# Expert stage of a retention and mixture-of-experts kernel: tile pairs outside, Strassen up projection, transposed down projection

## What is computed

```python
x = _layernorm(x + retention_stack(x))            # (8, 512, 256)
logits = xt @ Wr + br                             # xt: (4096, 256)
gates = entmax_bisect(logits)                     # (4096, 8)
gates = where(gates > THRESH, gates, 0)
h = relu(einsum('td,edf->etf', xt, W1) + b1[:, None, :])   # f = 1024
y = einsum('etf,efd->etd', h, W2) + b2[:, None, :]
out = einsum('etd,te->td', y, gates)
x = _layernorm(x + out)
```

## Time and profile before

| | |
|---|---|
| median of 3 runs | 2757.17 us (2754.56 to 2759.98) |
| profiled execution, span | 2757.3 us |
| expert stage, from its first instruction | 1210.8 us to the end |
| TensorE busy, share of the span | 95% |
| VectorE, ScalarE, GpSimd busy | 49%, 49%, 47% |
| matmuls | 14962 |
| mean TensorE clock granted | 0.975 of full |

### The profile page before, as it was taken

The page is one execution under the profiler, slowest core; times in us unless marked ns, Lnnn a source line. Parts: engine busy times, 40 slices in busy tenths (PEclk is TensorE's granted clock), DMA queues, the critical chain, the costliest instruction groups (busy, mean ns, idle before and its releaser), DMA issues.

```text
span 2757.3 us, 42999 instructions
## 1 busy us (share of the span) xinstructions
PE 2625.7 (95%) x14962; PEld 2292.4 (83%) x14962; DVE 1348.6 (49%) x2432; ACT 1361.9 (49%) x2246; POOL 1301.5 (47%) x1142
## 2 busy tenths in 40 slices
PE   7999999999999999949899999999999999999998
PEld 5788778877888788738798998989989989899997
DVE  2677887777777877757812112121121121211233
ACT  3555555566556555525344444444444444444443
POOL 2244554455445544435345445454454454544454
PEclk8999999999999999966999999999999999999999
DMA  4110020002000100042001001000010000000000
GB/s 153 58 31 30 31 69 31 30 31 69 31 30 31 38 31 23 15 133 70 31 0 33 0 0 33 0 29 5 0 34 0 0 33 0 2 0 0 8 23 31
DMA packets 70774, 82.77 MB, mean 30 GB/s; under 512 B 3104, under 2 KB 65696, under 8 KB 70688
## 3 DMA queue, kind: packets, MB, share of 16 engines
q1 hardware_dynamic: 70560, 81.58, 9.0%
q10 hardware_dynamic: 128, 0.03, 0.0%
HBM read 58.27 MB, written 23.33 MB: 30 GB/s over the span
## 4 chain that ended last, share of the span: by engine, by line
issue 24%; POOL 17%; PE 13%; POOLq 1%; DVE 0%; DMA 0%; ACT 0%; ACTq 0%; DVEq 0%; SPq 0%
POOL hid_lo L1257 17%; PE m_ps L1500 4%; PE m_ps L1501 4%; PE m_ps L1502 4%; DMA xh<-h_store 0%; POOLq L1256 0%; PE m_ps L1519 0%; PE m_ps L1526 0%; DVE x L1358 0%; POOLq L1260 0%; ACT x1T_hi L1302 0%; ACT x1Tf L1301 0%; DVE xh L1370 0%; DVE m_stat L1347 0%; POOL rstd L1236 0%
## 5 line engine op out<-in xcount | busy, mean ns | idle before, releaser
L1257 POOL TENSOR_TENSOR hid_lo<-act,hid_hi 128x512 fp32r<-128x512 f32 x512 | 701.5, 1372 | 759.6 <-ACT act L1329 759.5
L1327 ACT ACTIVATE hid_hi<-m_ps,b_e 128x512 fp32r<-128x512 f32 x512 | 353.4, 690 | 811.4 <-PE m_ps L1502 811.2
L1444 DVE TENSOR_TENSOR tile_out<-m_ps,b_bc 128x512 f32<-128x512 f32 x128 | 82.4, 686 | 1015.9 <-PE m_ps L1502 1015.6
L1329 ACT ACTIVATE act<-m_ps,b_e 128x512 f32<-128x512 f32 x512 | 349.7, 683 | 0.0
L1500 PE MATMUL m_ps<-w_even,hid_hi 128*128 128x256 f32 x1024 | 289.6, 283 | 13.5 <-DVE tile_out L1444 13.0
L1502 PE MATMUL m_ps<-w_even,hid_lo 128*128 128x256 f32 x1024 | 290.3, 284 | 0.0
L1501 PE MATMUL m_ps<-w_even,hid_hi 128*128 128x256 f32 x1024 | 290.3, 283 | 0.0
L1500 PE MATMUL m_ps<-w_odd,hid_hi 128*128 128x256 f32 x1024 | 289.1, 282 | 0.8 <-POOL hid_lo L1257 0.6
L1502 PE MATMUL m_ps<-w_odd,hid_lo 128*128 128x256 f32 x1024 | 289.7, 283 | 0.0
L1501 PE MATMUL m_ps<-w_odd,hid_hi 128*128 128x256 f32 x1024 | 289.6, 283 | 0.0
L320 POOL TENSOR_TENSOR pf_lo<-tmp,pf_hi 128x512 fp32r<-128x512 f32 x128 | 161.8, 1298 | 159.4 <-ACT pf_hi L497 159.4
(11 more groups left out here) (176 smaller groups left out, 6305.4 us busy)
## 6 DMA issues: line engine op xcount, KB each, us to landing
h_store<-h_out SPq DMA_DIRECT2D x32, 512.0 KB, 3.2
raw<-in_L_ffn_W SPq DMA_DIRECT2D x16, 1024.0 KB, 6.8
h_in<-h_store SPq DMA_DIRECT2D x24, 512.0 KB, 4.3
h_in<-in_L_attn_x SPq DMA_DIRECT2D x8, 512.0 KB, 5.0
raw<-in_L_attn_Wf SPq DMA_DIRECT2D x8, 512.0 KB, 7.6
acc<-in_L_attn_x SPq DMA_DIRECT2D x8, 512.0 KB, 4.2
xh<-h_store SPq DMA_DIRECT2D x8, 512.0 KB, 5.0
out<-acc SPq DMA_DIRECT2D x8, 512.0 KB, 2.8
```

The lines of the kernel that those rows point to most:

```text
L1257: nc.gpsimd.tensor_tensor(out=hid[1][:, j % RING, :], in0=act32[:, j % FULL, :], in1=f32(hid[0][:, j % RING, :]), op=ALU.subtract).then_in ...
L1327: nc.scalar.activation(hid[0][:, j % RING, :], hid_bank(j), ACT.Relu, bias=bias)
L1329: nc.scalar.activation(act32[:, j % FULL, :], hid_bank(j), ACT.Relu, bias=bias).then_inc(hid_relu, 1)
L1444: nc.vector.tensor_tensor(out=tile_out[:, 2 * half:2 * half + 2, :], in0=out_half(parity_t, half).rearrange("p (k d) -> p k d", d=D), in1= ...
```

## The change

Only the expert stage changes (the semaphores of the weight halves in the retention layers become one count, in the same order of work). Four pairs of tiles run outside and the eight experts inside. A step, a "quad", is one pair of tiles, one expert and two hidden chunks: 128 quads in all, QPP = 32 for a pair, FP = 4 for an expert. The four blocks of a quad (two chunks by two tiles, each a sum over two halves of 128 features) come out of seven products instead of eight, after Strassen in the form of Winograd:

- of the weights VectorE makes four sums S1 to S4 of 128 by 128 (`sum_weights`) in the buffer into which they were loaded, ScalarE rounds 11 blocks (1408 columns) in one copy (`high_weights`), VectorE subtracts (`low_weights`); this is done for every quad, so for every pair of tiles again;
- of the tokens four sums T1 to T4 are made once for a pair (`sum_tokens`), with seven high and seven low halves;
- three banks take the products. ScalarE copies the first product to `first` (`keep_first`), VectorE makes `second` and `third` and three of the four blocks (`second_sum`, `third_sum`, `block_sum`), each from one PSUM bank and one SBUF tile;
- ReLU runs twice per block on ScalarE (`relu`), from PSUM for block C11 and from SBUF for C22, C21 and C12, and GpSimd subtracts (`low_hidden`);
- `down` has the weights stationary and the 512 columns of the hidden block moving: 24 matmuls of 512 columns for a quad, with features on the output's partitions;
- the gate must then be a row over tokens: the gates are transposed, stored to memory and loaded as broadcast rows (`gate_bc`). VectorE adds the bias and multiplies (`gate_out`), GpSimd adds into `acc` (`add_expert`), one of 512 columns for each quad on the mean;
- moments, transposes, scores and the 25 bisection steps of the next pair run inside the windows of the present one; for the first pair, four steps come ahead and three in each of the first seven windows.

Window w issues the products of quad w+1 between the down projections of quad w. The diff, shortened, with all that the prediction speaks of; first two helpers of VectorE:

```diff
-            for j in range(AHEAD):
-                up(w1[0], 0, 0, j)
-            for e in range(2):
-                expert(e, e)
...
+            def sum_weights(q):
...
+                one = chained(nc.vector.tensor_tensor(out=part(8), in0=part(0), in1=part(2), op=ALU.add))
+                nc.vector.tensor_tensor(out=part(10), in0=part(1), in1=part(0), op=ALU.subtract)
+                dve.wait_ge(dve_done, one)
+                landed(nc.vector.tensor_tensor(out=part(9), in0=part(8), in1=part(1), op=ALU.subtract))
+                nc.vector.tensor_tensor(out=part(11), in0=part(3), in1=part(9), op=ALU.subtract).then_inc(w_summed, 1)
...
+            def block_sum(q, k):
+                p, e, fp = quad(q)
+                done, src, other, made = {C22: (4, bank_d, third, 2), C21: (6, bank_b, first, 3), C12: (7, bank_d, second, 4)}[k]
+                dve.wait_ge(up_done, 7 * q + done)
...
+                nc.vector.scalar_tensor_tensor(out=full[:, k, :], in0=src, scalar=b1_col(e, 2 * fp + BLOCK_ROW[k]), in1=other[:, :],
+                                               op0=ALU.add, op1=ALU.add).then_inc(sums, 1)
```

The loop over windows on VectorE:

```diff
+            for w in range(-1, QUADS):
+                p, i = w // QPP, w % QPP
+                if w >= 0 and w % FP == 0 and w:
+                    for j in (2, 3):
+                        gate_out(w // FP - 1, j)
+                if w + 1 < QUADS:
+                    second_sum(w + 1)
+                if w + 3 < QUADS:
+                    low_weights(w + 3)
+                if w < CLOSED:
+                    bisect(EARLY + PER_WINDOW * (w + 1) + 1)
...
+                if w + 1 < QUADS:
+                    third_sum(w + 1)
+                    block_sum(w + 1, C22)
+                if w + 4 < QUADS:
+                    sum_weights(w + 4)
+                if w < CLOSED:
+                    for n in range(2, PER_WINDOW + 1):
+                        bisect(EARLY + PER_WINDOW * (w + 1) + n)
...
+                    if 18 <= i < 31:
+                        bisect(2 * (i - 18) + 1)
...
+                if w >= 0 and w % FP == FP - 1:
+                    for j in (0, 1):
+                        gate_out(w // FP, j)
+                if w + 1 < QUADS:
+                    block_sum(w + 1, C21)
+                    block_sum(w + 1, C12)
```

The same on ScalarE, in the same loop:

```diff
+                if w + 3 < QUADS:
+                    high_weights(w + 3)
+                if w + 1 < QUADS:
+                    keep_first(w + 1)
+                if w >= 0:
+                    relu(w, C12)
...
+                if w + 1 < QUADS:
+                    for k in (C11, C22, C21):
+                        relu(w + 1, k)
```

On GpSimd:

```diff
+                if w >= 0:
+                    low_hidden(w, C12)
...
+                if w >= FP * 2:
+                    add_expert(w // FP - 1, w % FP)
+                if w + 1 < QUADS:
+                    for k in (C11, C22, C21):
+                        low_hidden(w + 1, k)
```

On TensorE, where a product of quad w+1 stands ahead of each down projection of quad w, and then the waits inside `product`:

```diff
+                for n in range(5):
+                    if ups:
+                        product(w + 1, n)
+                    if downs:
+                        down(w, n // 2, n % 2)
...
+                    down(w, C21, 1)
+                if ups:
+                    product(w + 1, 5)
+                if downs:
+                    down(w, C12, 0)
+                if ups:
+                    product(w + 1, 6)
+                if downs:
+                    down(w, C12, 1)
...
+                if n in (1, 2) and q:
+                    pe.wait_ge(sums, 5 * (q - 1) + 3 + n)
+                if n == 3:
+                    pe.wait_ge(sums, 5 * q + 1)
```

More of the change, by code:

```diff
@@ new lines, in expert_mixture @@
+        t_sum = sb("t_sum", [P, 4, S])
+        acc = [sb(f"m_acc{s}", [P, DC, 2 * S]) for s in range(2)]
+        gate_bc = [sb(f"gate_bc{s}", [P, 2 * S]) for s in range(2)]
+        gate_first = sb("gate_first", [P, 2 * S])
+        hid_hi, hid_lo = (sb(f"hid_{n}", [P, 4, S], F32R) for n in ("hi", "lo"))
+        first, second, third = (sb(f"sum{n}", [P, S]) for n in range(3))
+        full = sb("full", [P, 4, S])
+        gated = sb("gated", [P, 4, S])
+        xs, hs = (sb(f"m_{n}s", [P, 2, TB, D]) for n in ("x", "h"))
@@ new lines, in add_expert @@
+            def add_expert(n, j):
+                at = acc[n // E % 2][:, j % 2, (j // 2) * S:(j // 2 + 1) * S]
+                if n == 1:
+                    pool.wait_ge(first_added, j + 1)
+                else:
+                    pool.wait_ge(acc_added, added(n - 1, j))
+                pool.wait_ge(out_gated, 4 * n + j + 1)
+                nc.gpsimd.tensor_tensor(out=at, in0=at, in1=gated[:, j, :], op=ALU.add).then_inc(acc_added, 1)
+            for t in range(2):
+                inverse_root(t)
@@ new lines, in relu @@
+            def relu(q, k):
+                p, e, fp = quad(q)
+                bias = b1_col(e, 2 * fp + BLOCK_ROW[k])
+                if k == C11:
+                    act.wait_ge(up_done, 7 * q + 5)
+                    src = bank_a
+                else:
+                    act.wait_ge(sums, 5 * q + {C22: 3, C21: 4, C12: 5}[k])
+                    src = full[:, k, :]
+                if q:
+                    act.wait_ge(hid_used, 4 * (q - 1) + k + 1)
+                if k == C11:
+                    nc.scalar.activation(hid_hi[:, k, :], src, ACT.Relu, bias=bias)
+                    if q:
+                        act.wait_ge(hid_ready, 4 * (q - 1) + k + 1)
+                    nc.scalar.activation(full[:, k, :], src, ACT.Relu, bias=bias).then_inc(relu_ready, 1)
+                else:
+                    nc.scalar.activation(hid_hi[:, k, :], src, ACT.Relu)
+                    nc.scalar.activation(full[:, k, :], src, ACT.Relu).then_inc(relu_ready, 1)
@@ L1400, in each @@
+            mx, lo, total, step = (tau[:, n, :] for n in range(4))
+            SPAN = 1.0 - float(E) ** -0.5
             def each(v):
                 return v.unsqueeze(2).to_broadcast([P, NB, E])
-            fixed = B * TILE_CHAIN
-            count[0] = 0
-            mx, lo, total, above, sign, step, tot = (ent_s[:, i, :] for i in range(7))
-            scores, work = gates[:, :, :], ent_w
-            SPAN = 1.0 - float(E) ** -0.5
-            def rowsum_of_squares(ahead):
-                landed(nc.vector.scalar_tensor_tensor(out=work, in0=scores, scalar=ahead, in1=each(lo), op0=ALU.subtract, op1=ALU.subtract), fixed)
-                landed(nc.vector.scalar_tensor_tensor(out=work, in0=work, scalar=0.0, in1=work, op0=ALU.max, op1=ALU.mult), fixed)
-                landed(nc.vector.tensor_reduce(out=total, in_=work, op=ALU.add, axis=AX.X), fixed)
@@ new lines, in second_sum, with third_sum @@
+            def second_sum(q):
+                dve.wait_ge(up_done, 7 * q + 2)
+                dve.wait_ge(s1_ready, q + 1)
+                if q:
+                    dve.wait_ge(sums, 5 * (q - 1) + 5)
+                nc.vector.tensor_tensor(out=second[:, :], in0=bank_b, in1=first[:, :], op=ALU.add).then_inc(sums, 1)
+            def third_sum(q):
+                dve.wait_ge(up_done, 7 * q + 4)
+                nc.vector.tensor_tensor(out=third[:, :], in0=bank_b, in1=first[:, :], op=ALU.add).then_inc(sums, 1)
@@ new lines, in _, with block_of @@
+            last = PAIRS * E - 1
+            add_last(last, 0)
+            add_last(last, 1)
+            for j in (2, 3):
+                gate_out(last, j)
+                add_last(last, j)
+            for t in range(2):
+                def block_of(k):
+                    return ps[:, 2 * t + k // 2, (k % 2) * D:(k % 2 + 1) * D]
+                dve.wait_ge(z_psum, t + 1)
+                moments(block_of, z_moments(PAIRS - 1, t))
+                normalise(lambda k: hs[:, t, k, :], block_of, z_moments(PAIRS - 1, t), z_ready)
@@ new lines, in down @@
+            def down(q, k, dh):
+                p, e, fp = quad(q)
+                n = q // FP
+                j = 2 * BLOCK_TILE[k] + dh
+                opens = k in (C11, C22)
+                if dh == 0:
+                    pe.wait_ge(hid_ready, 4 * q + k + 1)
+                if fp == 0 and opens:
+                    if n:
+                        pe.wait_ge(out_gated, 4 * (n - 1) + j + 1)
+                    else:
+                        pe.wait_ge(xT_kept, 4)
+                at = (W2_ODD if BLOCK_ROW[k] else W2_EVEN) + dh
+                ins = mm3(out_bank(j), [h[:, q % RING, cols(at)] for h in (w_hi, w_lo)], [h[:, k, :] for h in (hid_hi, hid_lo)],
+                          fp == 0 and opens, fp == FP - 1 and not opens)
+                if dh:
+                    ins.then_inc(hid_used, 1)
+                elif fp == FP - 1 and not opens:
+                    ins.then_inc(out_psum, 1)
@@ L1608, in build @@
+            for j in range(4):
+                transpose_z(PAIRS - 1, j)
 def build(nc, x, Wkqv, Wm1, bm1, Wm2, bm2, gn_g, gn_b, Wf1, bf1, Wf2, bf2, ln_g, ln_b,
```

843 lines of the change are left out of this document (452 added, 391 removed).

## The result

| | before | after |
|---|---|---|
| median | 2755.95 us (2754.56 to 2759.98, 4 runs) | 2935.06 us (2933.74 to 2936.38, 4 runs) |
| ratio, 95% interval | | 1.065 [1.064, 1.066] |
| profiled span | 2757.3 us | 2934.7 us |
| TensorE, VectorE busy | 95%, 49% | 88%, 78% |
| ScalarE, GpSimd busy | 49%, 47% | 52%, 54% |

The account below looks back on a forecast made before the run. The changed kernel was taken as bound by a loop through VectorE, ScalarE and GpSimd, lengthened by VectorE-GpSimd conflicts: first `second_sum` ends at 1253, 127 passes take 1687, the end 25, giving 2965 us; range 2690 to 3050.

Parts of the forecast that it names:

- TensorE's part: Matmuls of a quad: 45 of 512 columns at 0.232 us, 10.44 us against 11.28, 108 us less in 128 quads.
- The ring: Loop from C21 sum through ScalarE, VectorE and GpSimd to the next: 11.7 us with conflict, 8.9 without.
- S: End of a `second_sum` on VectorE, from which a pass is timed; the first forecast at 1253 us, the last at 2940.
- ScalarE's share: From C21's end to next S: two ReLU 1.15, copy 1.28, `keep_first` 0.60, then `second_sum` 0.68; 3.7 us.
- the run of GpSimd's instructions: `add_expert`, then subtractions of C11 and C22, three in a row until S + 6.9, weight sums passing one by one between.
- Gates: Two `gate_out` on VectorE ahead of C21 in 29 passes: 1.3 us each, 38 us.
- Steps: Bisection steps of pairs 2 to 4: 75 at 1.18 us, start and end 2 each, 95 us.
- The first seven: First seven passes, three bisection steps each, no `add_expert`, subtractions falling on the steps: 13.6 us each, 95 us.
- conflicts cost nothing: Rival: VectorE and GpSimd do not delay each other, TensorE bounds plain windows; 2693 us, chance 0.20.
- The pass under 10.5 us that two instructions would give: Rival: two of GpSimd's instructions get in between, not three; plain passes stay at 10.44 us, total 2800, chance 0.20.
- the change does less than it says: Rival on the matmul count, rejected in the forecast since the instruction order shows 45 of 512 columns; no chance given.
- The clock: Rival: TensorE's clock falls when idle, up to 7 us more in 46 windows, 320 us, total 3285; chance 0.05.

Follow-up runs that it names:

- the doubled product: Each quad's first product issued twice, the second overwriting it, 48 matmuls of 512 columns a quad, against the changed kernel; 2935.4 us.
- the best version: Changed kernel with weight sums ahead of `second_sum`, `keep_first` ahead of the 1408-column copy, two gated sums between C21 and C12; 2748.52 us, 0.998 of before.

## Why the prediction was right

- **TensorE's part.** 45 matmuls of 512 columns a quad, at 0.227 us instead of 0.232: 10.2 instead of 10.44. It decided nothing in the changed kernel, as the doubled product shows, and in the best version it sets the plain passes but not those with steps. The 216 ns that the prediction sets beside its rows is, in the section of the Trainium skill that it names (TensorE: Matmul & The Clock Gate, Back-to-back issue gap), the figure for a matmul by itself and not for a stream of weight loads and matmuls; no term of the sum used it.
- **The ring.** Plain passes 11.39 us against 11.7. All points are there in the trace: first weight sum at S + 2.9 (2.8 forecast), C12's subtraction over at S + 2.7 (2.75), the add at S + 3.9 (4.1), C22's subtraction at S + 6.5 (6.9), C21 at S + 7.7 (8.0), ScalarE's share 3.7 (3.7). The mis-sized term is the run of GpSimd's instructions: the add ended 0.2 sooner than I had it, and the two behind it follow in 2.64 us together, where I had given 1.4 to each. 118 x 0.31 is 37 us, more than the whole miss of 30; the other terms nearly cancel.
- **Why it does not recover.** The plain passes stay at 11.4 in the run with only the first and last step as well, and between the gates of the last pair, where no bisection is near. The forecast had it that a pass of 10.44 us just holds until something makes it late. That is not shown: with the add and the weight sums in their places no pass of the changed kernel was under 11.3.
- **Gates** 12.7 against 11.39, so 1.3 as forecast. **Steps** 13.8 with two, 1.2 each against 1.18; behind the weight sums most of them ran unhindered, as that price supposed. **The first seven** 97.7 in all against 95. All 127 passes took 1653 us against 1687.
- **The ends.** First S at 1252.0 (1253), last S to the end 29.6 us against 25.
- **The rivals.** That conflicts cost nothing fell by the durations above. The pass under 10.5 us that two instructions would give occurs three times in 127: once (10.3) just before the add begins, and in the last two passes (9.2 and 10.2), where no weight sums are left to be held up and ScalarE has no 1408 columns to copy. All three fit the theory; in the first the missing add is the only difference. That the change does less than it says fell by the count of matmuls. The clock fell in part, below; its 320 us did not come.

A detail was off: I put TensorE's wait at product 3 for L1549, with 1 us or more. It is 0.7 there (59.6 us in 90 waits), and as much or more is waited for the block sums L1562.

What I had not seen: that the ring is so easily opened. I took the weight sums' place in the queue as given and priced it well, but these four small instructions put ahead of `second_sum` give back 163 of the 179 us. With GpSimd's subtractions shortened the time is 2674 us; no order of instructions got there, and that all of the way from 2749 to 2674 is hold-ups is likely but not shown. A version with the bisection spread over more windows was not tried.

## What to carry to other kernels

Before a method that trades matmuls for sums, follow one pass around every engine and not only each engine's total: here none was over 87% busy and the kernel still lost 6.5%. Put instructions that can be held up (small, SBUF only, not urgent) where their engine waits anyway, and never between two steps of the ring that sets the pace. When work is moved for that reason, list what the other engine runs at the new place first; three of these experiments (both with the steps behind C12, and the first step behind `low_weights`) failed because three or four instructions ran where I had counted fewer.

## What was unexpected of the hardware

- TensorE's clock falls to its lower level, 1.2 GHz, for short stretches and comes back. Between 1300 and 2912 us there are 27 of them, 109 us in all; 16 begin within some 2 us behind a wait of 1.9 to 3.1 us. TensorE in time:

```profile
1955.59 0.47 PE L1671 MATMUL m_ps<-hid_hi,m_w_hi 128*128 128x512 f32 x1 [3.06 <-DVE gated L1575]
...
1956.81 0.64 PE L1671 MATMUL m_ps<-m_t_hi,m_w_hi 128*128 128x512 f32 x1 [0.29 <-DVE full L1562]
1957.26 0.63 PE L1672 MATMUL m_ps<-m_t_lo,m_w_hi 128*128 128x512 f32 x1
...
1960.57 0.40 PE L1671 MATMUL m_ps<-hid_hi,m_w_hi 128*128 128x512 f32 x1
1960.80 0.39 PE L1672 MATMUL m_ps<-hid_lo,m_w_hi 128*128 128x512 f32 x1
```

Starts lie 0.43 to 0.45 us apart there, then 0.23 again. At half the clock 109 us hold at most 55 us of extra time; how much of it was on the path was not measured, and since a ring of other engines sets the pace it is probably little. From 1677 to 1850 us there is none, with passes of 11.4 to 14.6 us and TensorE busy for 87%.

- In a chain of small dependent instructions one is held up by each GpSimd instruction that it meets, however short it is itself: the comparison of a bisection step, 0.17 us alone, took 0.92. So the price of a chain goes by the number of GpSimd's instructions that it meets, not by its length. The step's reduction, the only one of the five that is a `tensor_reduce`, was not held up once in 100 (0.22 us at most), nor in any experiment; the forecast had counted it with the rest.
- Of the 67 MB more by DMA, 50 are the reloading of weights for each pair (256 loads of 256 KB against 16 of 1024 KB) and 16 the gate rows (31 loads of 512 KB). They cost next to nothing: from 1347 to 2912 us the DMA share is 0.17 and no engine waits for a weight load, one waits once, 6.2 us, for a gate row, and the best version moves the same 149.4 MB.
